# Loop over image couples written out, no one-column products, and a forward transform in half height in a fused convolution and spectral block

## What is computed

```python
# layer 0: 3x3 convolution with binary weights (sign times alpha)
x = x + conv3x3(_gn(x), sign(L0_conv_weight) * L0_conv_alpha)
# layer 1, on n = _gn(x)
h  = einsum('oc,bchw->bohw', w_in, n)          # 64 -> 256 channels
hp = 8 x 8 patches of h
hp = irfft2(rfft2(hp) * fft_filt)               # per patch and channel
h  = depthwise_conv3x3(h, w_dw)
x1, x2 = split(h, 2, axis=1)
x  = x + einsum('oc,bchw->bohw', w_out, gelu(x1) * x2)
```

## Time and profile before

| | us |
|---|---|
| median of 3 runs | 5864.78 |
| lowest of the runs | 5864.78 |
| highest of the runs | 15798.39 |
| profiled execution | 5862.9 |
| its span, first to last instruction | 5861.1 |

### The profile page before, as it was taken

How to read it: one execution, slowest core, us unless ns; L and a number is a source line. 1 busy time by engine, 2 the same in 40 slices (tenths; PEclk the granted TensorE clock), 3 DMA queues, 4 the chain that set the end, 5 groups by cost and what they waited for, 6 DMA issues and landing times.

```text
span 5861.1 us, 168822 instructions
## 1 busy us (share of the span) xinstructions
PE 5594.5 (95%) x66244; PEld 3466.6 (59%) x66244; DVE 4876.2 (83%) x6181; ACT 3315.5 (57%) x4194; POOL 3787.1 (65%) x2055
## 2 busy tenths in 40 slices
PE   6999999999999999999999999999999999999998
PEld 3665656556565565655656556565565656656665
DVE  6888888888887888888888888888888888888877
ACT  3655555555565555655555555565655555556565
POOL 3766666666666666666666666666666666666676
PEclk9999999999999999999999999999999999999999
DMA  2001010010101001010010100101001010010000
GB/s 95 17 19 66 18 61 24 34 48 18 65 20 49 33 18 65 20 49 36 18 64 18 50 35 18 64 21 52 30 18 64 21 52 30 21 64 18 21 23 27
DMA packets 43895, 217.60 MB, mean 37 GB/s; under 512 B 5238, under 2 KB 6104, under 8 KB 36952
## 3 DMA queue, kind: packets, MB, share of 16 engines
q1 hardware_dynamic: 43096, 206.45, 9.0%
HBM read 103.67 MB, written 102.76 MB: 35 GB/s over the span
## 4 chain that ended last, share of the span: by engine, by line
PE 80%; DVE 11%; issue 5%; DMA 2%; DVEq 1%; ACT 1%; POOL 0%; SPq 0%; ACTq 0%; POOLq 0%
PE PS L896 20%; PE PS L913 19%; PE PS L860 14%; PE PS L886 13%; PE PS L876 6%; PE PS L926 6%; DVE v L633 6%; PE PS L869 2%; DVE g L656 2%; DVE PS L649 1%; DMA Xb<-in_x 1%; DVE hf L626 1%; ACT carry L462 1%; PE PS L848 0%; DMA out_x<-Xb 0%
## 5 line engine op out<-in xcount | busy, mean ns | idle before, releaser
L345 POOL TENSOR_TENSOR v_lo<-v,v_hi 128x1024 f16<-128x1024 f32 (+1 forms) x1792 | 3360.3, 1895 | 1935.5 <-ACT v_hi L441 1932.3
L633 DVE TENSOR_TENSOR v<-PS,smul 128x1024 f32<-128x1024 f32 (+1 forms) x1792 | 1905.4, 1085 | 380.1 <-PE PS L896 307.2
L441 ACT ACTIVATE v_hi<-v 128x1024 f16<-128x1024 f32 (+1 forms) x1792 | 1652.2, 944 | 853.9 <-DVE v L633 607.4
L896 PE MATMUL PS<-hf,c_nodes 64*128 64x512 f32 (+1 forms) x7168 | 1735.0, 576 | 61.9 <-DVE v L633 37.8
L913 PEld LDWEIGHTS PS<-c_ext,v_hi 128*128 128x128 f16 x14336 | 1132.8, 98 | 487.6 <-issue 292.9
L913 PE MATMUL PS<-c_ext,v_hi 128*128 128x100 f16 (+2 forms) x14336 | 1261.7, 203 | 41.2 <-ACT carry L462 34.9
L913 PE MATMUL PS<-c_ext,v_lo 128*128 128x100 f16 (+2 forms) x14336 | 1253.9, 203 | 0.0
L913 PEld LDWEIGHTS PS<-c_ext,v_lo 128*128 128x128 f16 x14336 | 1120.1, 97 | 1.2
L626 DVE TENSOR_TENSOR hf<-PS,mult 128x1024 f32<-128x1024 f32 (+1 forms) x896 | 963.1, 1087 | 176.3 <-PE PS L886 163.9
L896 PEld LDWEIGHTS PS<-hf,c_nodes 64*128 64x128 f32 x7168 | 574.3, 185 | 671.2 <-issue 406.9
L886 PE MATMUL PS<-win_sb,xf 64*128 64x256 f32 x6272 | 866.6, 403 | 67.8 <-DVE hf L626 50.2
(11 more groups left out here) (67 smaller groups left out, 3853.8 us busy)
## 6 DMA issues: line engine op xcount, KB each, us to landing
out_x<-Xa SPq DMA_DIRECT2D x96, 448.0 KB, 2.5
out_x<-Xb SPq DMA_DIRECT2D x96, 448.0 KB, 2.5
Xa<-in_x SPq DMA_DIRECT2D x16, 2240.0 KB, 10.8
Xb<-in_x SPq DMA_DIRECT2D x16, 2240.0 KB, 10.9
Xa<-in_x SPq DMA_DIRECT2D x8, 1344.0 KB, 6.0
Xb<-in_x SPq DMA_DIRECT2D x8, 1344.0 KB, 7.1
out_x<-Xa SPq DMA_DIRECT2D x8, 504.0 KB, 3.1
out_x<-Xb SPq DMA_DIRECT2D x8, 504.0 KB, 2.6
```

The source lines that it names most:

```text
L345: nc.gpsimd.tensor_tensor(v_lo[:, img, :, k0:k1, :], v32[:, V_BUF[kind(b, s)][img][grp], :, 0:k1 - k0, :], v_hi[:, img, :, k0:k1, :], ALU. ...
L441: nc.scalar.activation(v_hi[:, img, :, k0:k1, :], v32[:, V_BUF[kind(b, s)][img][grp], :, 0:k1 - k0, :], ACT.Copy).then_inc(act_vhi[img], 1)
L633: nc.vector.tensor_tensor(v32[:, V_BUF[kind(b, s)][img][grp], :, 0:k1 - k0, :], PS[:, bank:bank + 2, 0:(k1 - k0) * C2].rearrange("p i (k c ...
L896: last = nc.tensor.matmul(PS[:, bank + side, 0:(k1 - k0) * C2], c_nodes[half, :], hf[half, img, k0:k1, :].rearrange("p k c -> p (k c)"), s ...
```

## The change

Four edits:

1. The loop of 7 rounds with two couples is replaced on every engine by the same calls in Python, one for each couple from 1 to 14.
2. The product with a single column ahead of each convolution strip is gone. Its waits go to the strip's first product.
3. `xn` holds the strip patch by patch (14 patches of 8 x 8), no longer block by block. After the transposes a patch's 64 pixels lie on one half of the partitions. `c_fwd` has 64 columns, the basis twice below one another, and *forward_transform* makes, per block, two products of 64 rows, one for each half, each with 64 moving columns and into a bank of its own. *spectrum* gathers the two banks into `xf`, which keeps its layout.
4. Two memsets of one column on VectorE per couple, ahead of `bn_aggr`, are gone.

```diff
-        c_fwd = sb("c_fwd", [BPX, BPX])
+        c_fwd = sb("c_fwd", [BPX, P * P])
-        xn = sb("xn", [128, NBLK, ROWS, BW])
+        xn = sb("xn", [128, 2 * NBLK, P, P])
...
-            with sp.Fori(0, (PAIRS - 2) // 2) as two:
-                image(sp.snap(two * 2 + 1), 1, True, True, True)
-                image(sp.snap(two * 2 + 2), 0, True, True, True)
+            for n in range(1, PAIRS - 1):
+                image(n, n % 2, True, True, True)
...
-                nc.scalar.activation(xn[:].rearrange("p k r c -> p r k c"),
-                                     X[par][:, s * ROWS:(s + 1) * ROWS, :].rearrange("p r (k c) -> p r k c", c=BW),
+                nc.scalar.activation(xn[:].rearrange("p q r c -> p r q c"),
+                                     X[par][:, s * ROWS:(s + 1) * ROWS, :].rearrange("p r (q c) -> p r q c", c=P),
...
-                nc.scalar.activation(xf[:].rearrange("p k f -> p (k f)"), flat(bank, NBLK * BPX), ACT.Copy).then_inc(act_xf, 1)
+                nc.scalar.activation(xf[:].rearrange("p k (s f) -> p s k f", f=P * P),
+                                     PS[:, bank:bank + 2, 0:NBLK * P * P].rearrange("p s (k f) -> p s k f", f=P * P),
+                                     ACT.Copy).then_inc(act_xf, 1)
...
-                nc.vector.memset(agg_wait[:], 0.0)
...
-                nc.tensor.matmul(PS[0:C, bank, 0:1], csign[:, 0, :], S_hi[:, 0, 0:1], start=True, stop=True, skip_group_check=True)
...
                     last = nc.tensor.transpose(flat(bank, NBLK * 128)[:, k * 128:(k + 1) * 128],
-                                               xn[:, k].rearrange("p r c -> p (r c)"), c_id[:])
+                                               xn[:, 2 * k:2 * k + 2].rearrange("p q r c -> p (q r c)"), c_id[:])
...
-                    last = nc.tensor.matmul(flat(bank, NBLK * BPX)[:, k * BPX:(k + 1) * BPX], xT[:, k, :], c_fwd[:],
-                                            start=True, stop=True)
+                    for side in range(2):
+                        half = slice(side * P * P, (side + 1) * P * P)
+                        last = nc.tensor.matmul(PS[:, bank + side, k * P * P:(k + 1) * P * P], xT[half, k, :], c_fwd[half, :],
+                                                start=True, stop=True)
```

More of the change, by code:

```diff
@@ L74, in shape_constants @@
     basis, picks = patch_basis()
-    px = [(r * BW + patch * P + s) for patch in range(2) for r in range(P) for s in range(P)]
-    forward = np.zeros((BPX, BPX))
     pick = np.zeros((P * (P // 2 + 1), BPX))
     for patch in range(2):
-        at = px[patch * P * P:(patch + 1) * P * P]
-        forward[np.ix_(at, range(patch * P * P, (patch + 1) * P * P))] = basis
         for f, (a, b) in enumerate(picks):
@@ L94, in shape_constants @@
     pair = np.kron(np.eye(HC // 2), np.full((2, 2), 0.5))
-    return {"forward": forward, "pick": pick, "pair": pair, "apart": np.eye(HC) - pair, "identity": np.eye(HC),
+    return {"forward": np.concatenate([basis, basis]), "pick": pick, "pair": pair, "apart": np.eye(HC) - pair, "identity": np.eye(HC),
             "nodes": np.concatenate([nodes, nodes]), "taps": taps, "ext": ext}
@@ L172, in build @@
         bn = sb("bn", [128, 2 * STRIPS, 6])
-        agg_wait = sb("agg_wait", [128, 1])
         mvx = sb("mvx", [128, 2])
@@ L389, in _ @@
             image(0, 0, False, True, True)
-            with pool.Fori(0, (PAIRS - 2) // 2) as two:
-                image(pool.snap(two * 2 + 1), 1, True, True, True)
-                image(pool.snap(two * 2 + 2), 0, True, True, True)
+            for n in range(1, PAIRS - 1):
+                image(n, n % 2, True, True, True)
             image(PAIRS - 1, 1, True, True, False)
@@ L547, in _ @@
             image(0, 0, False, True, True)
-            with act.Fori(0, (PAIRS - 2) // 2) as two:
-                image(act.snap(two * 2 + 1), 1, True, True, True)
-                image(act.snap(two * 2 + 2), 0, True, True, True)
+            for n in range(1, PAIRS - 1):
+                image(n, n % 2, True, True, True)
             image(PAIRS - 1, 1, True, True, False)
@@ L824, in _ @@
             image(0, 0, False, True, True)
-            with dve.Fori(0, (PAIRS - 2) // 2) as two:
-                image(dve.snap(two * 2 + 1), 1, True, True, True)
-                image(dve.snap(two * 2 + 2), 0, True, True, True)
+            for n in range(1, PAIRS - 1):
+                image(n, n % 2, True, True, True)
             image(PAIRS - 1, 1, True, True, False)
@@ L1166, in _ @@
             image(0, 0, False, True, True)
-            with pe.Fori(0, (PAIRS - 2) // 2) as two:
-                image(pe.snap(two * 2 + 1), 1, True, True, True)
-                image(pe.snap(two * 2 + 2), 0, True, True, True)
+            for n in range(1, PAIRS - 1):
+                image(n, n % 2, True, True, True)
             image(PAIRS - 1, 1, True, True, False)
```

## The result

The changed kernel takes 5728.36 us in the median of 4 runs (5726.52 to 5729.65), against 5864.78 us: a ratio of 0.9768, 95% interval 0.9749 to 0.9788. That is 136 us less (124 to 147 by the interval) where 130 were forecast against the median (128 worked out from the profile), and 2.3% where 2.2% stood. (The one run of 15798.39 us of the kernel before is not in the ratio.)

A forecast was written before the change was run, and what follows sets the result against it. TensorE was taken to bound conv steps, TensorE and VectorE in turn plain steps, a load's wait the turns. 45 + 39 + 44 = 128 us off the profiled 5862.9 gave 5735 us, range 5708 to 5779.

The forecast's parts named there:

- Part 1: Loop over couples written out: register operations and separate waits go, 3.2 us in each of 14 couples, 45 us less.
- the turns: Stretch from step 13 of a couple to the next one's step 0: written-out loop saves 0.25 us each (0 to 0.5).
- upper bound of 53: The most, in us, that Part 1 was given to save; its lower bound was 35.
- Part 2: One-column product ahead of convolution strips gone: 36 us over 105 conv steps, up to 3 before the first couple, 39 together.
- conv step: Steps 6 to 12 of a couple, with two convolution strips of the next; TensorE nearly full; forecast 28.52 to about 27.6 us.
- upper bound of 45: The most, in us, for Part 2, should the slow first group with its 0.39 us go too; lower bound 0.
- Part 3: Forward transform in half height: fewer changes of array form, 0.42 us in each of 105 conv steps, 44 us (0 to 50).
- plain steps: A couple's other seven steps; TensorE and VectorE wait in turn; forecast 21.91 to 21.5 us, with 0 from Part 3.
- third rival: In the forward transform, half-height products really go twice as fast: 5710 us, chance 0.08.
- The room behind it: Slack left behind the transform in a conv step after saving 0.42 us: GpSimd's buffer 0.24, ScalarE's carry 0.3, evaluation 0.4.
- first rival: In conv steps another wait, GpSimd's buffer or ScalarE's carry, takes Part 3's place: 5779 us at most, chance 0.14.
- The load's wait: VectorE's first statistics of the next couple wait up to 7.5 us for their load; change over 1 us per couple refutes.

The follow-up runs named there:

- one-half run: Changed kernel with both half-height products of a forward-transform block on the lower 64 rows of the array: 6185.68 us, ratio 1.055.
- 128-column run: Changed kernel with each half-height product of the forward transform streaming 128 columns instead of 64: 5727.81 us, ratio 0.9768.
- sister kernels: Two kernels: changed kernel plus a product with one moving column ahead of each forward transform, of 128 rows (5793.87 us) or 64 rows (5760.04 us).
- loop: Kernel before the change with only the loop over couples written out: 5811.91 us, ratio 0.9914.
- one-column: Kernel before the change with the loop written out and the one-column products gone as well: 5767.99 us, ratio 0.984.
- half height alone: Kernel before the change, loop and one-column products kept, with only the forward transform in half height: 5806.08 us, ratio 0.9901.

## Why the prediction was right

**Part 1, 45 us.** Measured alone 52 us, 41 of them in the steps from 0 to 13, where the reading of couple 0 against couple 5 gave 42. Couple 0 was a sound sample of the whole: step for step couples 1 to 14 took its times. At the turns I allowed 3.5 us for all of them and 12.6 went in that kernel, but this can't be put down to the loop: with the half-height transform and the loop kept, 8 us went there too. My upper bound of 53 had no working either; its pieces give (2.47 + 0.5 + 0.5) x 14 = 49.

**Part 2, 39 us.** Measured 44 on top of part 1. The term was 0.34 us a conv step; it was 0.37, for the second strip's slow first group (0.39 us) went with the break. Its successor now starts 0.19 us behind it where it was 0.22, which is the 0.03; the upper bound of 45 had allowed 0.06. Ahead of the first couple it was 3.6 us for 3.

**Part 3, 44 us.** Measured 46 us in the steps, and 40 in the medians on top of the other two. A little of the agreement is luck: in conv steps, for which all of it was forecast, 40 to 42 us went, and in the plain steps, for which I put 0 with bounds of 6, it was 4 to 7. The stretch from L888 to L905 was worked out as 3.03 us and is 3.05. The pieces of it hold: the halves work in pairs, 0.112 us apart (one-half run), the columns make no difference (128-column run), and the changes of form are most of what was saved (sister kernels, 0.30 us). The third rival, half-height products at twice the speed, falls: from first to last record the transform takes 1.40 us where it took 1.55, not 0.8. The Trainium skill's "Up to 2×" for a contraction of 64 rows (TensorEngine Tiling (Array Packing), section Theoretical Speedup) was not to be had here, where every product has weights of its own.

**The room behind it.** GpSimd had been the narrowest with 0.24 us left. In the timelines of GpSimd and VectorE:

```profile
2116.55 2.13 POOL L339 TENSOR_TENSOR v_lo<-v,v_hi 128x1024 f16<-128x1024 f32 x1 [6.40 <-ACT v_hi L436]
...
2119.02 1.23 DVE L625 TENSOR_TENSOR v<-PS,smul 128x1024 f32<-128x1024 f32 x1 [0.60 <-PE PS L888]
```

The buffer is free at 2118.68 and VectorE takes it at 2119.02, released by TensorE: 0.34 us are left. The first rival, another wait in its place, falls for that reason. It is still what would come next: a further saving of that size in this place would begin to run into it. The load's wait, on which no row gave a hold, went from 97 to 93 us in 14 turns, well within the 1 us per couple that was allowed.

**The sum.** 128 us stood against the profiled execution's 136. The steps give: couples 1 to 14, 120.8 us; couple 0, 5.7; couple 15, 0.9; ahead of the first couple 3.9; the turns 5.1. Of the 8 us that were missing, some 4.5 are part 2's (43.6 us of steps and start against 39: the slow group, and 1.5 us in the first step of couple 0, which the transform took back), 2 are part 3's (46 against 44), and 1.6 the turns' (5.1 against 3.5).

**What stays open** are the turns. Their sum over 14 was 423 us in the kernel before and 411, 414, 415, 418, 422, 419 and 413 us in seven others that didn't touch them (in the order: loop, one-column, half height alone, changed kernel, 128 columns, and the two sisters). Each turn has the load's wait and a stretch at half clock, of 3.4 to 10.2 us, and where that begins against the work differs from turn to turn. That this is all of the difference wasn't shown. So no part of the 12 us between the highest and the lowest is shown to come from an edit.

## What to carry to other kernels

A float32 product whose weights are used once took about 0.11 us a record here, with 64 moving columns as with 128; look at the spacing of the load records before counting columns. Count the changes of array form in a hand-written order: two of them cost 0.30 us in the sister kernels, and a product of a single column in a form of its own cost 0.12 to 0.25 us. Where part of a program is written out and part is looped, the trace has the price of the loop in it already.

## What the runs showed of the hardware

The granted clock fell to half, 1.2 GHz, at the end of a stretch in which TensorE was busy without a break, but on one half of the array alone: in the one-half run it was 0.60 of full in the 3 us from 2293, where the transform ends, and the mean over the kernel 0.956, against 0.989. In 125 of its 224 strips a stretch at half clock begins between 1.2 us before and 0.4 us behind the end of the transform; the changed kernel has none there. And the halves do not wait for one another in the order of the program: in the same run an L888 product starts at 2293.37, ahead of the lower half's last L868 at 2293.48, which stands before it in the program. The product that went ahead is the group's second, on the upper half, which had nothing to do: its second record, which carries the group's semaphore, starts 0.33 us ahead of the other's.
